# Attention with scores and values side by side on TensorE, and VectorE's rotation right behind the maxima

## The reference

```
x = x + 0.5 * moe(layernorm(x))        # 64 experts, 8 of them per token
x = x + attention(layernorm(x))        # 16 heads of 64
x = x + 0.5 * moe(layernorm(x))        # the same weights

attention(x):
    q, k, v = split(x @ w_qkv.T)
    q = q*cos + rotate_half(q)*sin + fenc          # k the same
    p = softmax(q @ k.T / 8)
    return (p @ v) @ w_out.T + b_out
```

## Time and profile before

| what | value |
|---|---|
| median of three runs | 913.99 us |
| the profiled execution's own time | 914.71 us |
| its span in the profile | 912.7 us |
| TensorE busy over the span | 850.9 us (93%) |
| VectorE, ScalarE, GpSimd busy | 568.5, 503.8, 494.3 us |
| granted TensorE clock, mean | 0.97 |

### The profile page before, as it was taken

One profiled execution on the slowest core, in us unless ns is written; L12 is line 12 of the kernel. 1 busy time (PEld: TensorE's weight loads), 2 busy tenths in 40 slices (PEclk: granted clock), 3 DMA queues, 4 the chain that ended last, 5 costly groups with the idle time before them and its releaser, 6 DMA issues.

```text
span 912.7 us, 18913 instructions
## 1 busy us (share of the span) xinstructions
PE 850.9 (93%) x6328; PEld 745.5 (82%) x6328; DVE 568.5 (62%) x1736; ACT 503.8 (55%) x1376; POOL 494.3 (54%) x536
## 2 busy tenths in 40 slices
PE   5989989999964999999999999999979999999977
PEld 4889989999963777777777777777679999999962
DVE  7947753333336878888888888877543376433446
ACT  4423333333321888888888888888832333333336
POOL 4156777777762222256666666666657354444440
PEclk9779999999995999999999999999999999999999
DMA  9947877776626890000000000000050588888756
GB/s 327 368 160 225 258 231 227 236 242 218 205 87 227 197 151 1 1 14 27 23 25 25 25 25 25 22 19 15 6 211 18 182 313 284 279 287 291 241 190 259
DMA packets 65150, 140.70 MB, mean 154 GB/s; under 512 B 10223, under 2 KB 37296, under 8 KB 63940
## 3 DMA queue, kind: packets, MB, share of 16 engines
q1 hardware_dynamic: 53316, 118.59, 39.9%
q0 software_dynamic: 11776, 21.39, 7.5%
HBM read 107.72 MB, written 35.56 MB: 157 GB/s over the span
## 4 chain that ended last, share of the span: by engine, by line
PE 62%; POOL 13%; issue 6%; DVE 5%; ACT 4%; DMA 4%; DVEq 0%; ACTq 0%; POOLq 0%; SPq 0%
PE ps L1387 12%; PE ps L1962 6%; POOL y_rows L589 6%; POOL f_xg L578 6%; PE ps L1987 6%; PE ps L1406 6%; PE ps L615 5%; PE ps L1974 5%; PE ps L72 4%; PE ps L1947 3%; PE ps L2002 3%; PE ps L73 2%; PE ps L74 2%; ACT at_prob L2263 2%; PE ps L655 2%
## 5 line engine op out<-in xcount | busy, mean ns | idle before, releaser
L1856 POOL TENSOR_TENSOR at_m<-at_m 128x512 f32<-128x512 f32 x64 | 81.5, 1274 | 147.8 <-DVE at_m L2079 147.8
L1181 POOL DMA_INDIRECT xs_rows<-xr,slots_of x128 | 127.4, 995 | 43.8 <-issue 32.1
L2263 ACT ACTIVATE at_prob<-ps,at_nmax 128x256 f32<-128x256 f32 x256 | 118.0, 475 | 39.2 <-DVE at_nmax L2086 38.8
L1365 POOL DMA_INDIRECT y_rows<-f_og,f_put x80 | 81.7, 1021 | 95.6 <-ACT f_og L1518 76.1
L878 DVE TENSOR_TENSOR f_ehid<-f_esil,ps 128x480 f32<-128x480 f32 (+1 forms) x80 | 50.8, 634 | 116.0 <-ACT f_esil L719 107.9
L1657 DVE TENSOR_TENSOR f_hid<-f_sil,ps 128x480 f32<-128x480 f32 (+1 forms) x80 | 50.7, 634 | 107.0 <-ACT f_sil L1511 100.4
L1387 PE MATMUL ps<-f_xgT,f_ring 128*128 128x160 f32 x768 | 115.0, 299 | 1.7 <-issue 1.7
L615 PE MATMUL ps<-f_xgT,f_ring 128*128 128x160 f32 x768 | 114.9, 299 | 0.2 <-issue 0.2
L719 ACT ACTIVATE f_esil<-ps 128x480 f32<-128x480 f32 (+1 forms) x80 | 44.4, 555 | 120.8 <-PE ps L615 120.8
L1511 ACT ACTIVATE f_sil<-ps 128x480 f32<-128x480 f32 (+1 forms) x80 | 44.4, 555 | 118.8 <-PE ps L1387 118.8
L1387 PEld LDWEIGHTS ps<-f_xgT,f_ring 128*128 128x128 f32 x768 | 107.0, 190 | 2.1 <-issue 2.1
(11 more groups left out here) (256 smaller groups left out, 1844.2 us busy)
## 6 DMA issues: line engine op xcount, KB each, us to landing
f_ring<-in_wexp SPq DMA_DIRECT2D x128, 576.0 KB, 4.6
y_rows<-zeros SPq DMA_DIRECT2D x16, 512.0 KB, 6.2
f_yt<-y_rows SPq DMA_DIRECT2D x4, 2048.0 KB, 8.5
at_yt<-y_rows SPq DMA_DIRECT2D x6, 1024.0 KB, 4.9
xs_rows<-at_blank SPq DMA_DIRECT2D x16, 342.5 KB, 10.0
f_xg<-xs_rows SPq DMA_DIRECT2D x16, 342.5 KB, 3.3
y_rows<-f_og,f_put POOLq DMA_INDIRECT x160, 2.7
y<-y_rows SPq DMA_DIRECT2D x4, 512.0 KB, 4.4
```

The lines of the kernel that those rows point to most:

```text
L1181: nc.gpsimd.indirect_dma_start(xs_dram, bass.IndirectOffsetOnAxis(s.slots_of[:, t, k:k + 1], 0), s.xr[:, t, :], None, bounds_check=last_sl ...
L1365: nc.gpsimd.indirect_dma_start(ydram, bass.IndirectOffsetOnAxis(put[:, n:n + 1], 0), og[:, g, c, :], None, bounds_check=last_row, oob_is_e ...
L2263: mm = nc.scalar.activation(prob[:, p % 2, h, t, :], ps[:, SB + h, t * SEQ:(t + 1) * SEQ], ACT.Exp, bias=nmax[:, p % 2, h, t:t + 1], accum ...
```

## The change

On TensorE `values` goes directly behind `scores`, then `turn`, `turn_p`, `project`, the v projection, the matmuls of the routing, and last the projection of q and k. `qkv` is split into `project_v` and `project_qk`. On VectorE `rotate` goes behind the two maxima (and the residual), and what it rotates there is the pair u+2, whose q and k were projected in the slot before. GpSimd's `add` follows it. The routing's matmuls write into the first score bank instead of VB and wait for the exponentials of head 0; ScalarE reads them between its two copies of the turned probabilities, and TensorE waits for that copy before the scores of the next slot. ScalarE copies the values' result before q and k. The bias moves from slot 3 to slot 5.

```diff
-        LN_STATS, LN_MEAN, LN_APPLY, LN_BIAS = 0, 1, 2, 3
+        LN_STATS, LN_MEAN, LN_APPLY, LN_BIAS = 0, 1, 2, 5
...
-                        if there(b, p, -AHEAD, False, last):
-                            add(*pair(b, p, AHEAD))
+                        if there(b, p, 1 - AHEAD, False, last) and not (first and p == 0):
+                            add(*pair(b, p, AHEAD - 1))
...
                 def room(b, p):
                     u = PAIRS * b + p
-                    pe.wait_ge(vev, min(u + AHEAD, PAIRS * BATCH) if isinstance(u, int) else u + AHEAD)
-                    pe.wait_ge(oev, u - VLAG)
-                    return ps[:, VB, 0:TPB * P]
+                    pe.wait_ge(ex, 2 * u + 1)
+                    return ps[:, SB, 0:TPB * P]
...
+                        if p == 1 and kind in (MIDDLE, LAST):
+                            pe.wait_ge(s.room_r, 3 * (b - 2) + 3)
+                        if p == PICK_TURN + 1 and not first:
+                            pe.wait_ge(s.room_r, 3 * (b - 1) + 1)
+                        if p == PICK_LOGITS + 1 and not first:
+                            pe.wait_ge(s.room_r, 3 * (b - 1) + 2)
                         scores(b, p)
+                        if there(b, p, VLAG, first, last):
+                            values(*earlier(b, p, VLAG), ending)
+                        if there(b, p, -1, first, last):
+                            turn(*pair(b, p, 1))
+                        if there(b, p, 1, first, last):
+                            turn_p(*earlier(b, p, 1), 0, ending)
+                            turn_p(*earlier(b, p, 1), 1, ending)
+                        if there(b, p, JLAG, first, last):
+                            project(*earlier(b, p, JLAG), not last, not there_is_v)
+                        if p == LN_TURN and not last:
+                            turn_x(b + 1, False)
+                        if there_is_v:
+                            if p + AHEAD == PAIRS:
+                                pe.wait_ge(xx, b + 2)
+                            project_v(*nxt, xs)
                         if p == 0 and kind in (MIDDLE, LAST):
                             pick_ranks(nc, pe, s, room(b, p), b - 2)
...
+                        if there_is_v:
+                            project_qk(*nxt, xs)
...
                         maximum(b, p, 1)
                         if p == RES_AT and not first:
                             residual(b - 1)
+                        if there(b, p, 1 - AHEAD, first, last) and not (first and p == 0):
+                            rotate(*pair(b, p, AHEAD - 1))
                         invert(b, p, 0)
                         normalise(b, p, 0)
...
-                        if there(b, p, -AHEAD, first, last):
-                            rotate(*pair(b, p, AHEAD))
...
                         exps(b, p, 0)
                         exps(b, p, 1)
+                        if there(b, p, VLAG, first, last):
+                            take_o(*earlier(b, p, VLAG))
                         if there(b, p, -1, first, last):
                             take_qk(*pair(b, p, 1))
-                        if there(b, p, VLAG, first, last):
-                            take_o(*earlier(b, p, VLAG))
                         if there(b, p, 1, first, last):
                             take_p(*earlier(b, p, 1), 0)
+                        if p == 0 and kind in (MIDDLE, LAST):
+                            pick_take_ranks(nc, act, s, ps[:, SB, 0:TPB * P], b - 2)
...
+                        if there(b, p, 1, first, last):
                             take_p(*earlier(b, p, 1), 1)
                         normalise(b, p, 1)
```

More of the change, by code:

```diff
@@ L1843, in load_cur @@
                 def load_cur(b):
-                    after(pool, vp, PAIRS * b)
+                    after(pool, qk, PAIRS * b)
                     pool.wait_ge(xx, b + 1)
@@ L1868, in batch @@
                 def batch(b):
-                    last = b == BATCH - 1
+                    first, last = b == 0, b == BATCH - 1
                     for p in range(PAIRS):
-                        if there(b, p, -AHEAD, False, last):
-                            add(*pair(b, p, AHEAD))
+                        if there(b, p, 1 - AHEAD, False, last) and not (first and p == 0):
+                            add(*pair(b, p, AHEAD - 1))
                         if p == LN_MEAN and not last:
@@ L1916, in _, with project_qk @@
             def _(pe):
[L1917 removed]
+                def project_qk(b, p, xs):
                     u = PAIRS * b + p
@@ L1924, in qkv, with project_v @@
                     mm.then_inc(qk, 1)
+                def project_v(b, p, xs):
+                    u = PAIRS * b + p
                     taken = u - AHEAD - VLAG + 1
@@ L1966, in scores, with turn_p @@
                                 mm.then_inc(sc, 1)
-                def turn_p(b, p, h):
+                def turn_p(b, p, h, alone=True):
                     u = PAIRS * b + p
                     pe.wait_ge(pn[h], u + 1)
-                    after(pe, pte, 2 * u + h - 1)
+                    if alone:
+                        after(pe, pte, 2 * u + h - 1)
                     for t in range(TPB):
@@ L2015, in batch @@
                     for p in range(PAIRS):
-                        scores(b, p)
+                        ending = last and p + AHEAD > PAIRS
+                        there_is_v = p + AHEAD < PAIRS or not last
+                        nxt, xs = pair(b, p, AHEAD), xcur if p + AHEAD < PAIRS else xnext
+                        if p == 1 and kind in (MIDDLE, LAST):
[4 more added lines that the diff above has]
+                            pe.wait_ge(s.room_r, 3 * (b - 1) + 2)
+                        scores(b, p)
+                        if there(b, p, VLAG, first, last):
[13 more added lines that the diff above has]
+                            project_v(*nxt, xs)
                         if p == 0 and kind in (MIDDLE, LAST):
@@ L2050, in _ @@
                 pe.wait_ge(xx, 1)
-                qkv(0, 0, xnext)
-                qkv(0, 1, xnext)
+                project_v(0, 0, xnext)
+                project_qk(0, 0, xnext)
+                project_v(0, 1, xnext)
+                project_qk(0, 1, xnext)
                 turn(0, 0)
-                qkv(0, 2, xnext)
+                project_v(0, 2, xnext)
+                project_qk(0, 2, xnext)
                 pe.wait_ge(xc, 1)
@@ L2154, in split @@
                     v.wait_ge(xev, b + 1)
-                    after(v, vp, PAIRS * (b - 1) + AHEAD)
+                    after(v, qk, PAIRS * (b - 1) + AHEAD)
                     after(v, xc, b)
@@ L2288, in batch @@
                     for p in range(PAIRS):
[L2289 to L2294, removed]
                         exps(b, p, 0)
                         exps(b, p, 1)
+                        if there(b, p, VLAG, first, last):
+                            take_o(*earlier(b, p, VLAG))
                         if there(b, p, -1, first, last):
                             take_qk(*pair(b, p, 1))
-                        if there(b, p, VLAG, first, last):
-                            take_o(*earlier(b, p, VLAG))
                         if there(b, p, 1, first, last):
                             take_p(*earlier(b, p, 1), 0)
+                        if p == 0 and kind in (MIDDLE, LAST):
+                            pick_take_ranks(nc, act, s, ps[:, SB, 0:TPB * P], b - 2)
+                        if p == PICK_TURN and not first:
+                            pick_take_x(nc, act, s, ps[:, SB, 0:TPB * P], b - 1)
+                        if p == PICK_LOGITS and not first:
+                            pick_take_logits(nc, act, s, ps[:, SB, 0:TPB * P], b - 1)
+                        if there(b, p, 1, first, last):
                             take_p(*earlier(b, p, 1), 1)
```

## The result

| kernel | median, us | runs | ratio to before, 95% interval |
|---|---|---|---|
| before, same chip | 914.4 | 912.7 to 916.4 | |
| after | 936.3 | 933.0 to 936.9 | 1.023 [1.020, 1.026] |

The account below looks back on a forecast made before the run. TensorE's list bounds the attention; with the stop, the wait for v's copy and VectorE's list lengthen slots. 914.7 + 10.4 (slots 3 to 60) + 1.1 (tail) = 926.2, less 0.7 to the median: 925.5 us, range 912 to 931.

Parts of the forecast that it names:

- TensorE without waits: Slots 3 to 60 in the new order without VectorE's stop: 323.4 us against 332.6, 9.2 us less.
- rival A: GpSimd's sum merely shares with VectorE's products, as with the maxima; whole about 907.5 us; chance 0.15.
- The stop: GpSimd's sum holds VectorE's head 0 product until 0.11 us behind the sum's end; loss L, 1.0 us a slot.
- Rival B: GpSimd's sum stops VectorE only in part, 0.7 us instead of 1.0; whole 915 us; chance 0.09.
- turning point of 0.7: Stop in us a slot at which slots 3 to 60 take the old length, 332.6, and gain turns to loss.
- The way to TensorE: Head 1's reciprocal late at 5.84, ScalarE's product at 6.05, copy of v done at 7.27, next slot's values wait.
- pair sum of 11.53 us: Two neighbouring slots with the stop: 7.33 plus 4.20 us on TensorE, 5.77 a slot against 5.63 before.
- signs of being wrong: Forecast wrong if VectorE's head 0 product stays near 0.35 us, or if slots 4 and 7 are under 5.6.
- the size of the stop in the heavy slots: VectorE's list bounds slots with long small work, stop 1.0 us each: batch 48.2 us against 46.3, batches 2 to 5 +8.1.
- rival C: GpSimd's indirect DMAs also stop VectorE's small work, or values wait longer; 3 to 5 us more, 929 to 931; chance 0.15.
- Head and tail: First three slots 0 (at most 0.3 us); slots 61 and 62 wait for the routing copy, +0.7 and +0.4.
- The range: Whole kernel between 912 us, the slow end of the gainers, and 931, the top of the extra-loss rival.

Follow-up runs that it names:

- e8: e4, with GpSimd's sum in slots 0, 1, 2 and 4 also waiting for VectorE's small work there; 906.8 us, ratio 0.9936.
- e2: The changed kernel, with GpSimd's sum waiting for the head 1 reciprocal of its slot; 914.5 us, ratio 1.0002.
- e6: The changed kernel, with GpSimd adding only the first 256 of 512 columns; 912.6 us, ratio 0.9993.
- e3: The changed kernel, with ScalarE's copy of v ahead of its product for head 1; 926.9 us, ratio 1.015.
- e7: The changed kernel, with GpSimd's indirect DMAs of batches 0 to 5 moved behind its last slot; slots 3 to 60 345.2 us, whole 1036 (not read).
- e4: The changed kernel with the edits of both e2 and e3; 911.2 us, ratio 0.9969.
- e1: The changed kernel, with VectorE's rotation (pair three ahead) last in the slot again, GpSimd's sum beside the next maxima; 918.9 us, ratio 1.0055.

## Why the prediction was half right

**TensorE without waits, and rival A.** It gave 323.4 us for slots 3 to 60 without a stop and 907.5 for the whole. e8, in which few stops are left, has 324.2 and 906.8. The plain slots are 5.43 in e2, which has the forecast's order, and 5.40 in e8 (forecast 5.41 and 5.43). Right. That the totals agree within a microsecond is in part luck: e8 also copies v earlier, which the forecast did not have, and still has a stop of 1 us in slots p = 4. Rival A itself is refuted: the sum did not share with these products, e2 alone shows it.

**The stop.** L = 1.0 us from one product of 0.617 us beside a DMA; measured 1.06 in plain slots, the product ending 0.15 to 0.16 behind the sum (forecast 0.11). Shown by e2 (gone when the sum waits) and e6 (follows its length). Rival B's smaller stop did not come, but its turning point of 0.7 stands beside e6. The sum starts only 0.02 to 0.03 us ahead of the product, in the forecast as in the run. How this product fares when it is first, no run shows; in e8 the first of the norm's two instructions starts 0.22 us ahead of the sum (454.08 against 454.30) and takes its usual 0.34 us, and only the second stands.

**The way to TensorE.** Head 1's reciprocal, ScalarE's product, the copy of v, the values: as forecast, e3 prices it at 9.4 us. The pair sum of 11.53 us is 5.42 + 6.08 = 11.50 in slots 9 and 10. One of the prediction's signs of being wrong did come, slots 4 and 7 under 5.6: they take 5.40 and 5.45 in batches 2 to 5. The sign was set too high, for the prediction's own list has 5.60 and 5.52 there. Behind a long slot the next has its v in time and is short, so the loss shows in the slot before it.

**The step that failed is the size of the stop in the heavy slots: L = 1.0 a slot, in each of them.** In slots p = 2 and 4 of batches 2 to 5 it is 1.88 and 1.67, in p = 5 1.41 (a cast of GpSimd's, L1847, follows the sum and catches the second product), in p = 6 1.20. The prediction had a rival for the scatters, C, with 0.3 us in slots p = 1 and 4 beside the small work and 3 to 5 us in all. It looked at where GpSimd's scatters stand when VectorE is in time. But the stop makes VectorE late, the routing list is late with it, the scatters follow and run into the next product, and the sum comes right behind them. The lateness goes with the length of the stop: counted from the scores of slot 26 the list ends at 0.37 us before, 0.72 in e8, 1.50 with the half sum of e6, and 2.07 after; it is 2.06 in e7, so the scatters do not cause it. (In e2 and e4 it is 2.02: there the sum stops L2152, which stands ahead of the list.) e7 prices the scatter and the sum in a row: 7.0 of the 9.2 us between 343.0 and 352.2. By batches: 0 and 1 +0.4 and +1.9 (forecast +1.0, +1.3), 2 to 5 +16.3 (forecast +8.1; +10.4 in e7), 6 and 7 +1.0 and 0.0 (forecast +0.1, -0.1). The 2.2 us left lie mostly in slots p = 0 and 6 (6.48 and 6.68 in batch 3 of e7, forecast 6.15 and 6.35). For p = 6 the trace of e7 points at the cast: in slot 29 the pair of products takes 2.02 us instead of 1.66, 0.36 more, and the values of slot 30 wait for the copy of v behind it:

```profile
473.52 1.08 PE L1989 MATMUL ps<-at_pT,at_v 128*64 128x256 f32 x8 [0.87 <-ACT at_v L2253]
```

No run takes the cast away, and for p = 0 the cause stays open.

**Head and tail.** Slots 0 to 2 cost 1.2 us where I took 0: the values of slot 2 wait for the copy of v too (timeline of TensorE).

```profile
306.40 1.08 PE L1991 MATMUL ps<-at_pT,at_v 128*64 128x256 f32 x8 [1.60 <-ACT at_v L2255]
```

Slots 61 and 62 cost 1.16 and 0.40 (forecast 0.7 and 0.4). The first has the forecast wait for the routing copy,

```profile
668.18 0.49 PE L1965 MATMUL ps<-at_qkT 64*128 64x256 f32 x2 [0.46 <-ACT p_turned L1051]
```

and 0.4 of the copy of v, late behind a stop of 1.8 us in slot 60 that again has a scatter and the sum in a row: in e3, e4 and e8, where that copy is early, and in e7, where no scatter stands there, the slot takes 5.38, which is 0.74 over before. Together 19.6 + 1.2 + 1.6 = 22.4 against 21.7 between the two executions; of the difference, 0.4 lies ahead of slot 0, which after reaches that much earlier.

**The range.** Its upper end came from rival C's 3 to 5 us, a fixed extra for fixed places. The delays feed on one another, and a bound for that needs the walk with late lists, not the list in time.

## What to carry to other kernels

When an edit moves work of GpSimd beside other work of VectorE, read for each of these instructions where it reads and writes: what works beside sources in PSUM at no cost can stop the other engine for its whole length where both go from SBUF to SBUF (here 1.06 us a slot), and a single wait that lets VectorE pass first may be worth more than the edit. Two reorderings may each lose alone and gain together, so test the pair with the stall taken away before giving up either. And when VectorE becomes late, recompute when the queue that hangs on its results will run, instead of reading that from the trace of the kernel in time.

## What the runs showed of the hardware

- Between two instructions of GpSimd in a row (an indirect DMA to 454.21, the sum from 454.20) a product of VectorE that had started at 453.53 did not get in; it ended 0.16 us behind the second (the stop of 1.88 us above). This is no rule: in e6, with the half sum, the product in the same place ended 0.25 us behind the DMA's end, while the sum ran (0.84 us instead of 0.73), and only the second product stood until the sum was over.
- Beside an indirect DMA of GpSimd of about 1.0 us, with no sum behind it (kernel before), a product that starts up to 0.49 us into it takes 0.35 us as ever; one that starts later stands until 0.10 to 0.12 us behind its end. With the sum right behind, one that starts 0.30 us into it takes 2.16 us (after, slot 26).
- Beside GpSimd's sum, VectorE's TENSOR_SCALAR and TENSOR_TENSOR from SBUF to SBUF stood still even at two elements a partition (e4: L2152 1.21 us, against 0.17 in the changed kernel; L1145 1.22 against 0.27), and the maxima from PSUM were as fast beside it (0.682 us in e1) as without it (0.681 in the changed kernel). So was the aggregation of the routing norm's statistics (0.18 and 0.15 us for its two instructions, as in the kernel before), within a sum that ran from 450.32 to 451.59 (e4, slot 27):

```profile
450.77 0.25 DVE L1018 BATCH_NORM_AGGREGATE p_mv<-p_bst 128x2 f32<-128x6 f32 x2 [0.15 <-DVE p_bst L1013]
```

  The Trainium skill (SBUF — State Buffer, Who interferes with whom) has VectorE and GpSimd share one pair of ports by an exclusive lock that holds for a whole instruction; the stopped rows agree, the maxima too, and e6 does, by length.
- Scores and values side by side cost no more than other neighbours: where nothing waits (after, slot 52), the values' first record comes 0.31 us behind the last of the scores, as forecast; before, the turning's comes 0.31 behind it too.
